# Step 0 of a Strassen-Winograd FFN kernel reordered: weight units 0 to 3 back to back, transposes of A, gate and B between them

## What is computed

```python
def _L0_cond_ref(x, subjects, weights):      # x (32,128,2048), weights[idx] (128,128)
    return einsum('bct,bcd->bdt', x, weights[subjects])
def _L0_ffn_ref(x, W_base, b_base, W_gate, A, B):   # 2048 x 2048, E = 8, R = 16
    result = einsum('bnd,od->bno', x, W_base) + b_base
    probs = softmax(einsum('bnd,ed->bne', x, W_gate))
    route_w = the top 2 of probs, scaled to sum 1, as an (b,n,8) array
    h = einsum('bnd,erd->bner', x, A)
    delta = einsum('bner,eor->bno', h * route_w[..., None], B)
    return result + delta
out = x + _L0_ffn_ref(_L0_cond_ref(x, idx, cond_weights), W_base, b_base, W_gate, A, B)
```

## Time and profile before

| | |
|---|---|
| median of 3 runs | 1579.23 us (1577.51 to 1581.52) |
| the profiled execution: time | 1579.12 us |
| its span in the profile | 1577.3 us |
| TensorE busy | 1506.0 us, 95% |
| DVE, ACT, POOL busy | 1352.3, 626.1, 640.5 us |

### The profile page before, as it was taken

How to read it: one execution, slowest core, us unless ns; L and a number is a source line. 1 busy time by engine, 2 the same in 40 slices (tenths; PEclk the granted TensorE clock), 3 DMA queues, 4 the chain that set the end, 5 groups by cost and what they waited for, 6 DMA issues and landing times.

```text
span 1577.3 us, 25817 instructions
## 1 busy us (share of the span) xinstructions
PE 1506.0 (95%) x9411; PEld 808.5 (51%) x9411; DVE 1352.3 (86%) x2257; ACT 626.1 (40%) x1026; POOL 640.5 (41%) x508
## 2 busy tenths in 40 slices
PE   4678999999999999999989999999999999999998
PEld 4554554555455555555545455555455555455553
DVE  6788999999899999999968888888888888888875
ACT  6864444444543445434413332223332323332321
POOL 2565555666665555665522122122122122122122
PEclk9899999999999999999999999999999999999999
DMA  6234555655555555655797333344333344433342
GB/s 232 94 132 156 163 165 173 191 166 161 150 176 167 161 168 178 177 179 157 227 339 247 108 123 101 99 141 126 116 121 91 111 141 123 118 116 94 114 111 74
DMA packets 169567, 235.95 MB, mean 150 GB/s; under 512 B 71898, under 2 KB 88794, under 8 KB 167130
## 3 DMA queue, kind: packets, MB, share of 16 engines
q1 hardware_dynamic: 167426, 219.63, 46.0%
q10 hardware_dynamic: 2016, 14.68, 2.4%
HBM read 147.83 MB, written 86.43 MB: 149 GB/s over the span
## 4 chain that ended last, share of the span: by engine, by line
PE 73%; DVE 11%; issue 4%; POOL 2%; DMA 1%; ACT 1%; SPq 0%; DVEq 0%; ACTq 0%; POOLq 0%
PE bank_x L1427 8%; PE bank_x L1429 8%; PE bank_x L1428 8%; PE bank_y L1427 8%; PE bank_y L1429 8%; PE bank_y L1428 8%; PE bank_z L1427 3%; PE bank_z L1429 3%; PE bank_z L1428 3%; PE bank_h L1427 2%; PE bank_h L1429 2%; PE bank_h L1428 2%; PE bank_c L1427 2%; DVE t_sums L1070 2%; PE bank_c L1429 2%
## 5 line engine op out<-in xcount | busy, mean ns | idle before, releaser
L602 POOL TENSOR_TENSOR x_res<-x_res,t_sums 128x512 f32<-128x512 f32 x255 | 350.5, 1377 | 843.4 <-DVE t_sums L1075 684.1
L1427 PE MATMUL bank_y<-TT,s_parts 128*128 128x512 f16 x768 | 292.1, 380 | 4.7 <-DVE TT L1185 4.2
L1427 PE MATMUL bank_x<-TT,s_parts 128*128 128x512 f16 x768 | 292.9, 381 | 1.3 <-DVE TT L1185 1.3
L1428 PE MATMUL bank_x<-TT,s_parts 128*128 128x512 f16 x768 | 292.5, 381 | 0.0
L1429 PE MATMUL bank_x<-TT,s_parts 128*128 128x512 f16 x768 | 292.3, 381 | 0.0
L1429 PE MATMUL bank_y<-TT,s_parts 128*128 128x512 f16 x768 | 291.9, 380 | 0.0
L1428 PE MATMUL bank_y<-TT,s_parts 128*128 128x512 f16 x768 | 291.9, 380 | 0.0
L710 ACT ACTIVATE p_copies<-bank_x,y_inv 128x512 f32<-128x512 f32 x128 | 87.7, 685 | 417.7 <-PE bank_x L1429 307.3
L1075 DVE TENSOR_TENSOR t_sums<-t_sums,inv_w 128x512 f32<-128x512 f32 x255 | 233.8, 917 | 8.7
L1045 DVE TENSOR_TENSOR s_parts<-a_full,s_parts 128x512 f16<-128x512 f32 x224 | 192.9, 878 | 33.0 <-ACT s_parts L695 33.0
L574 POOL TENSOR_TENSOR x_res<-x_res,BT 128x512 f32<-128x512 f32 x128 | 206.9, 1616 | 26.3 <-DMA x_res<-in_x_dram 23.3
(11 more groups left out here) (243 smaller groups left out, 2750.5 us busy)
## 6 DMA issues: line engine op xcount, KB each, us to landing
x<-in_x_dram SPq DMA_DIRECT2D x32, 1024.0 KB, 5.8
x_res<-in_x_dram SPq DMA_DIRECT2D x128, 256.0 KB, 4.0
part_scratch<-x_res SPq DMA_DIRECT2D x128, 256.0 KB, 3.0
x_res<-part_scratch SPq DMA_DIRECT2D x128, 256.0 KB, 3.9
out_dram<-x_res SPq DMA_DIRECT2D x128, 256.0 KB, 3.0
wt_scratch<-late_words SPq DMA_DIRECT2D x64, 224.0 KB, 3.4
TT<-wt_scratch ACTq DMA_DIRECT2D x14, 1024.0 KB, 8.3
x_parts<-in_L_ffn_W_base_dram SPq DMA_DIRECT2D x18, 512.0 KB, 6.4
```

The source lines that it names most:

```text
L602: nc.gpsimd.tensor_tensor(XR[:, xr_slot(m), :], XR[:, xr_slot(m), :], TM[:, m % 2, :], ALU.add).then_inc(r_added, 1)
L1427: nc.tensor.matmul(dst, lhs[0], rhs[0], start=start, stop=False, skip_group_check=chained)
L1428: nc.tensor.matmul(dst, lhs[0], rhs[1], start=False, stop=False, skip_group_check=chained)
```

## The change

All of it is in step 0. On TensorE the units 1, 2 and 3 come before the conditioning quads and the products, with A's first transpose after unit 1, gate's and further transposes of A and B after unit 2, and the rest between quads and products. Gate is no longer scaled on DVE: 16 fp32 matmuls with a diagonal `gate_diag_f` transpose and scale it at once. For units 0 to 3 the casts of T2 and T4 move from ACT to GpSimd (a copy ahead of each low part). ACT sums the rows of unit 4 into another place, DVE makes the scales of unit 4 before the low parts of A12 to S3, and its first sum before B's low part. B's largest absolute value is taken by a DVE reduction (the scale was a sum on ACT). The load of B is issued after those of A and gate; the store of F before that of B. On ACT unit 7 is finished before x of step 1 is split; GpSimd does unit 0's low parts before it reorders B.

```diff
...
         agb_diag_f = h0[:, 0, 0:P]
+        gate_diag_f = h0[0:E, 1, 0:E]
         agb_diag_inv = h[:, :, :].rearrange("p b n -> p (b n)").bitcast(BF16)[:, 0:2 * P]
...
...
             load_x(0)
-            sp.dma_start(b_staged.rearrange("p (e n) -> p e n", e=E), b_rows).then_inc(b_in, 16)
             load_rows(1)
...
             sp.dma_start(g_staged, w_gate).then_inc(g_in, 16)
+            sp.dma_start(b_staged.rearrange("p (e n) -> p e n", e=E), b_rows).then_inc(b_in, 16)
             for g in range(2, NU // 2):
...
...
             load_rows(5)
+            sp.wait_ge(f_lo, 2)
+            sp.dma_start(ft_dram, FT_second.rearrange("p f s n -> p (f s n)")).then_inc(ft_out, 16)
             sp.wait_ge(b_lo, 1)
             sp.dma_start(bt_dram, BT_first).then_inc(bt_out, 16)
-            sp.wait_ge(f_lo, 2)
-            sp.dma_start(ft_dram, FT_second.rearrange("p f s n -> p (f s n)")).then_inc(ft_out, 16)
             sp.wait_ge(w_tr, 4 * 5)
...
...
                 for i, q in enumerate((T1, T3, T2, T4)):
-                    pool.wait_ge(w_sum_hi, 4 * g + i + 1)
+                    if g >= NU // 2:
+                        pool.wait_ge(w_sum_hi, 4 * g - NU + i + 1)
+                    elif q in (T1, T3):
+                        pool.wait_ge(w_sum_hi, 2 * g + i + 1)
+                    else:
+                        pool.wait_ge(w_sum, 4 * g + i + 1)
+                        link(nc.gpsimd.tensor_copy(t_dst(q, u, 0), quads(t_full(g, q))))
                     nc.gpsimd.tensor_tensor(t_dst(q, u, 1), quads(t_full(g, q)), t_dst(q, u, 0),
...
...
 
+            w_lower(0)
             pool.wait_ge(b_in, 16)
...
             part.then_inc(b_reordered, 1)
-            for g in range(4):
+            for g in range(1, 4):
                 w_lower(g)
...
...
                     junk_at = ((B22, B11) if g >= NU // 2 else (B11, T1))[i]
-                    ins = nc.scalar.activation(TT[:, junk_at, u // 4, :, :, u % 4 * P:(u % 4 + 1) * P],
+                    ins = nc.scalar.activation(SO[:, 7 + i, :, :, :].rearrange("p a c n -> p (a c) n") if g == NU // 2 else
+                                               TT[:, junk_at, u // 4, :, :, u % 4 * P:(u % 4 + 1) * P],
                                                rows_of(g, i).rearrange("p (a c n) -> p a c n", a=2, c=C4), ACT.Abs,
...
...
                 upper(g, 3, B21)
-                for i, q in enumerate((T1, T3, T2, T4)):
+                if g >= NU // 2:
+                    w_upper_sums(g, (T1, T3, T2, T4))
+
+            def w_upper_sums(g, made):
+                for i, q in enumerate(made):
                     act.wait_ge(w_sum, 4 * g + i + 1)
...
...
             sum_rows(0)
+            w_upper_first(0)
             sum_rows(1)
-            w_upper(0)
+            w_upper_rest(0)
+            w_upper_sums(0, (T1, T3))
             act.wait_ge(a_in, 16)
             nc.scalar.activation(junk[:, 0:T], a_staged, ACT.Abs, accum_out=agb_sum[:, 0:1]).then_inc(agb_sums, 1)
-            split_x_hi(0, 0)
-            split_x_hi(0, 1)
+            w_upper_first(1)
             act.wait_ge(g_in, 16)
...
                                  accum_out=agb_sum[0:E, 1:2]).then_inc(agb_sums, 1)
+            w_upper_rest(1)
             sum_rows(2)
+            w_upper_sums(1, (T1, T3))
             act.wait_ge(agb_spread, 1)
...
             copy_features(0)
-            w_upper(1)
-            lift_s(0, U_A11, A11)
-            copy_features(1)
-            sum_rows(3)
-            w_upper(2)
-            copy_features(2)
-            lift_s(0, U_S1, S1)
-            copy_features(3)
-            act.wait_ge(b_copied, 4)
-            nc.scalar.activation(BT_first[:, 0:O], b_transposed, ACT.Abs,
-                                 accum_out=agb_sum[:, 2:3]).then_inc(agb_sums, 1)
-            w_upper(3)
-            lift_s(0, U_A12, A12)
-            s_upper(0, S2)
-            lift_s(0, U_A22, A22)
-            sum_rows(4)
+            split_x_hi(0, 0)
+            split_x_hi(0, 1)
+            w_upper_first(2)
             act.wait_ge(g_tr, 1)
...
                                      ACT.Copy).then_inc(f_full, 1)
+            copy_features(1)
+            w_upper_rest(2)
+            sum_rows(3)
+            w_upper_sums(2, (T1, T3))
+            copy_features(2)
+            w_upper(3)
+            w_upper_sums(3, (T1, T3))
+            lift_s(0, U_A11, A11)
+            copy_features(3)
+            lift_s(0, U_S1, S1)
+            sum_rows(4)
+            lift_s(0, U_A12, A12)
+            s_upper(0, S2)
+            lift_s(0, U_A22, A22)
+            act.wait_ge(f_sum, 1)
+            split_f_hi(0, FT[:, :, :, :])
+            s_upper(0, S4)
+            s_upper(0, S3)
             act.wait_ge(agb_spread, 2)
             nc.scalar.copy(inv_b[:, :], BD[:, 0:ER]).then_inc(agb_inv, 1)
-            s_upper(0, S4)
-            s_upper(0, S3)
             nc.scalar.activation(BT_first[:, 0:O], b_transposed, ACT.Copy, scale=b_scale[:, 0:1]).then_inc(b_hi, 1)
-            act.wait_ge(f_sum, 1)
+            copy_p(0, 0, P1_COPY)
             act.wait_ge(cond_done, 4)
-            split_f_hi(0, FT[:, :, :, :])
-            copy_p(0, 0, P1_COPY)
             split_f_hi(1, FT_second)
...
...
             w_upper(6)
-            w_upper_first(7)
+            w_upper(7)
             split_x_hi(1, 0)
             split_x_hi(1, 1)
-            w_upper_rest(7)
             copy_p(0, 1, P1_COPY)
...
...
             def agb_scales(i, p=P):
-                dve.wait_ge(agb_sums, i + 1)
                 power_of_two(agb_pow2[0:p, :], agb_sum[0:p, i:i + 1], agb_clamped[0:p, :])
...
...
             find_maxima(0)
+            w_first_sum(0)
             find_top(0)
             w_scales(1)
-            w_sums_and_lower(0)
-            copy_b(0)
+            w_other_sums(0)
             scale_x(0)
-            split_x_lo(0, 0)
-            split_x_lo(0, 1)
+            dve.wait_ge(agb_sums, 1)
             agb_scales(0)
...
                                     ALU.mult, ALU.mult).then_inc(agb_diag, 1)
+            w_first_sum(1)
             dve.wait_ge(agb_diag, 1)
+            dve.wait_ge(agb_sums, 2)
             agb_scales(1, E)
+            nc.vector.tensor_scalar(gate_diag_f, ident[0:E, 0:E], agb_rpow2[0:E, :], TOP_A, ALU.mult, ALU.mult)
             nc.vector.tensor_scalar(agb_diag_inv[0:E, P:P + E], ident[0:E, 0:E], agb_pow2[0:E, :], 1.0 / TOP_A,
                                     ALU.mult, ALU.mult).then_inc(agb_diag, 1)
-            nc.vector.tensor_scalar(g_staged, g_staged, agb_rpow2[0:E, :], TOP_A,
-                                    ALU.mult, ALU.mult).then_inc(g_scaled, 1)
+            w_scales(2)
+            w_other_sums(1)
+            split_x_lo(0, 0)
+            split_x_lo(0, 1)
+            w_first_sum(2)
+            w_scales(3)
+            w_other_sums(2)
+            copy_b(0)
+            w_sums_and_lower(3)
+            s_lower(0, A11)
             copy_b(1)
-            w_scales(2)
-            w_sums_and_lower(1)
-            copy_b(2)
-            s_lower(0, A11)
-            w_scales(3)
-            w_sums_and_lower(2)
-            copy_b(3)
             s_lower(0, S1)
             sum_s2(0)
-            w_sums_and_lower(3)
+            w_scales(4)
+            s_lower(0, A12)
+            copy_b(2)
+            s_lower(0, S2)
+            sum_s4_s3(0)
+            s_lower(0, A22)
+            copy_b(3)
+            dve.wait_ge(b_copied, 4)
+            link(nc.vector.tensor_reduce(agb_sum[:, 2:3], b_transposed, AX_X, ALU.max, apply_absolute_value=True))
             agb_scales(2)
...
                                     ALU.mult, ALU.mult).then_inc(agb_diag, 1)
-            s_lower(0, A12)
-            s_lower(0, S2)
-            sum_s4_s3(0)
-            s_lower(0, A22)
             s_lower(0, S4)
             s_lower(0, S3)
-            w_scales(4)
+            w_first_sum(4)
             dve.wait_ge(b_hi, 1)
...
                                            in1=BT_first[:, 0:O], op0=ALU.mult, op1=ALU.subtract).then_inc(b_lo, 1)
-            w_first_sum(4)
             w_scales(5)
...
...
             spread_maxima(0)
-            transpose_b(0)
             w_quads(1)
-            transpose_b(1)
             pe.wait_ge(agb_diag, 2)
...
             transpose_a(0)
+            w_quads(2)
             pe.wait_ge(agb_inv, 1)
+            for c in range(16):
+                mm = nc.tensor.matmul(BC[:, c * E:(c + 1) * E], g_staged[:, c * P:(c + 1) * P], gate_diag_f,
+                                      start=True, stop=True)
+            mm.then_inc(g_tr, 1)
+            transpose_a(1)
+            transpose_b(0)
+            transpose_a(2)
+            w_quads(3)
+            pe.wait_ge(f_full, 2)
             cond(0, U_A11)
+            transpose_a(3)
+            transpose_b(1)
+            cond(0, U_S1)
+            product(0, 0, 0)
+            cond(0, U_A12)
             transpose_b(2)
-            transpose_a(1)
-            w_quads(2)
```

(17 more changed lines are left out.)

## The result

The changed kernel takes 1588.13 us (median of 5 runs, 1586.61 to 1588.29) against 1579.23 us before: ratio 1.0052, 95% interval 1.0041 to 1.0064, or 8.2 us slower (6.5 to 10.1). The prediction was 1573.5 us, range 1568.5 to 1580: wrong in its sign, and outside its range. The profiled execution spans 1586.3 us, 9.0 more than before.

What follows compares the result with a forecast made beforehand. TensorE is busy 95%, but step 0 is a web of short waits between ACT, DVE and GpSimd. Gains of 1.8 (unit 4) and 3.8 us (unit 7), 5.6 off 1579.12, gave 1573.5 us, range 1568.5 to 1580.

Steps and rivals of the forecast that it cites:

- First links: Step 0 to 38 us: unit 1 on TensorE 19.1 to 22.9, unit 2 from 30.1, likely at low clock, to 35.4.
- Gate: Sixteen fp32 matmuls replacing transposes on TensorE: 2.2 us, bounds 1.1 and 3.3, with ACT waiting, on the path.
- The chain that decides: DVE from unit 3's end to B's diagonal, ready at 65.8 to 68.1, taken as 67.4; 1.8 us won at unit 4.
- a little blocking: DVE's scales of unit 5 end at 80.9, where unit 4's other sums start instead of at 82.67.
- Rival 3: GpSimd's lock on DVE from 50 to 65 us: 8.7 us of blocking beyond that counted, 1582 us; chance 0.11.
- B's diagonal after 70: Sign of being wrong, in step 0: the diagonal was forecast at 67.4, with TensorE's wait ending near 67.5.
- The reduction: B's maximum on DVE, replacing ACT's 1.9 us pass by a reduction over 2048 elements: 2.28 us.
- After B: From B's diagonal to unit 4's other sums: B's low part 4.3 us to 79.0, unit 5's scales to 80.9.
- B's store: T4 of unit 4 waits for it until 82.9, nothing lost; rival 1 (0.22) had it possibly gating ACT there.
- Unit 7: Evacuations before x's halves: 2.7 us at product(0,1,1) plus 1.6 by full clock, 3.8 us won, bounds 2 and 4.5.
- Rival 4: Unit 4's scales come earlier but nothing uses them before 67.5, TensorE being parked; already in the sum, no chance given.
- Casts on GpSimd: T2 and T4 of units 0 to 3: two copies per unit at 0.57 us each, upper bound 1.14.

Runs made afterwards that it cites:

- the scales later: Changed kernel with DVE's scales of unit 4 moved back behind B's diagonal; ratio 1.0014 to the kernel before, +2.2 us.
- GpSimd held: Changed kernel with GpSimd waiting before T2 and T4 of unit 3 until B's diagonal is ready, DVE's order untouched; ratio 1.0062 to the kernel before, +9.8 us.
- the unparked run: Changed kernel with spread(4), unit 4's first quad and product(0,0,2) ahead of the spread of B's diagonal on TensorE; ratio 1.0059 to the kernel before, +9.3 us.
- the run with the casts on ACT: Changed kernel with the casts of T2 and T4 of units 0 to 3 back on ACT; ratio 1.0072 to the kernel before, +11.4 us.

## Why the prediction was wrong

The sum missed by 14.6 us (1588.1 against 1573.5). 11.5 of them stand at unit 4's other sums, 92.42 instead of 80.9.

- **First links: right, for one of two courses.** Counted were spread(1) at 19.1, unit 1 done at 22.9, A's and gate's diagonals at 26.7, unit 2's spread at 30.1; the execution with the scales later has 18.55, 22.7, 27.8 and 30.3. In the profile of the change unit 2's spread is at 32.72, by the clock in unit 0 and a diagonal that GpSimd held up; the count had neither: 2.4 us.
- **Gate: the size was off.** Counted 2.2 us with bounds 1.1 and 3.3; measured 3.73, outside the bounds, with the granted clock at 1.00 from end to end (38.6 to 42.3). The nearest row was that of sixteen transposes, doubled for the two entries of an fp32 matmul. There were two entries, but each took 0.117 us and not 0.07. The queue behind it was named rightly: ACT waits, then unit 3's row sums, then DVE. 1.5 us, plus 0.9 for a diagonal of unit 3's scales that took 1.19 instead of 0.28 beside GpSimd, plus about 0.9 in small hand-overs, which is what is left over: with the first links, 5.7 us late at the end of unit 3 (58.45, counted 52.7).
- **The chain that decides: the step that failed.** From there to B's diagonal 14.7 us were counted, with 1 us of blocking; it took 19.7. Unit 4's scales were put at 1.4 us, and "a little blocking" was allowed only for unit 5's; under a busy GpSimd they took 4.28, S2's low part 2.51, S4's sum 1.70. With GpSimd held this stretch takes 14.2. Rival 3 named this mechanism and the place; it priced eight two-input instructions at 7.8 us and left the scales out. The two-input ones lost about 4.5 us and the scales 2.9; 1.3 of these 7.4 lay over waits for ACT, which the held run shows (0.44 and 0.82). It gave 1582 by 8.7 us of blocking, which is more than this stretch lost; that it came nearest to the time is in part luck. Gate's size, the late course of the first links and unit 7's shortfall stood in no rival. B's diagonal after 70 was named as a sign of being wrong, and it came.
- **The reduction** took 2.29 us, as counted. The Trainium skill (SBUF — State Buffer, section Who interferes with whom) says that it never contends; the run with the scales later bears that out, with GpSimd at work from 66.34 to 70.2 and the reduction 2.29 at 67.89. The same section of the Trainium skill says that copies, casts and scalar operations of DVE can take the ports that it shares with GpSimd as well, under certain conditions. The 0.17 us instructions at 1.0 to 1.3 agree with that, and the prediction, which drew on this section only for instructions with two inputs, overlooked it.
- **After B: right but for 0.8 us, by two misses that cancel in part.** B's low part took 3.17 instead of 4.3, unit 5's scales 4.05 instead of 1.9 (GpSimd on the biases). B's store gated nothing.
- **Unit 7: right in kind, 3.8 counted, less won.** The idle at product (0,1,1) is 2.34 instead of 4.18 us, so 1.8 and not 2.7 (the 128x4 instruction, 1.00 us). The 1.6 of clock is absent in the change, where the low clock has moved to 130 to 135 us (0.74); where the order was changed alone it was 1.2. The first conditioning waited 0.3 us there. With 11.5 us lost up to unit 4's other sums, these and the small shifts behind them make up the 14.6.
- **Rival 4** was right that nothing uses unit 4's scales before B's diagonal; the unparked run shows that the converse, freeing TensorE, brings nothing either.
- **Casts on GpSimd:** four of the eight took 0.61 us, the others 1.07, 1.08, 1.15 and 1.61; the last two are above the upper bound of 1.14. They fall in units 0 and 1.

## What to carry to other kernels

Before a DVE instruction is moved, look at what GpSimd does at its new place: here a group of seven tiny instructions went from 1.4 to 4.3 us, a longer delay than any single large one had. The same group one diagonal later took 1.4 us, with DVE waiting 3.35 us for ACT soon behind it, and TensorE 1.1 for it. Where a chain of hand-overs sets the time, count the small operations at the price they have beside their new neighbours. Give an operation that the trace doesn't hold wide bounds: a similar one doubled was too low by a factor of 1.7. An engine that stands parked ahead of a wait is a symptom; what paid was to shorten the chain that ends the wait. And compare two profiles only after checking that both took the same course up to the edit.

## What the runs showed of the hardware

- A small DVE instruction can be held as long as a large one: over 128x2 one took 0.17 us beside an idle GpSimd and 1.12 to 1.27 beside a busy one, a 128x128 diagonal 0.28 and 1.12 to 1.20. Where the trace shows the GpSimd instruction beside a held one by itself, the held one ended within 0.1 us after it. The reciprocal over 128x2 between them, at 65.31 with GpSimd at work, was not held: 0.17. GpSimd in turn took 4.67 instead of 2.62 us for two additions.
- Sixteen fp32 matmuls of 8 columns (32 entries) took 3.73 us at a granted clock of 1.00, sixteen transposes of the same tiles 1.15. The loads of the stationary operand were busy 3.6 and 1.1 us of these, 32 of them and 16. In the run with the casts on ACT, where the clock was 0.57 for half of them, they took 4.64.
- One and the same order of work came in two courses, 2.1 to 2.6 us apart at unit 3's spread (46.96 to 47.46 or 49.55), with the granted clock of 20 to 25 us at 1.00 or 0.50.
